# Decay attention with seven quarter products for each pair of query, key and gate tiles, in a two-layer transformer kernel

## The reference, cut to what matters

```python
qkv = silu(hidden_states @ qkv_w.T)            # hidden_states: layernorm(x), K = 512
q, k, v = ...                                  # (b, 32 heads, 1024, 128) each
def step(kv, blk):                             # blocks of the sequence
    scores = einsum('bhnd,bhmd->bhnm', cq, ck) * diag_decay
    intra = einsum('bhnm,bhmd->bhnd', scores, cv)
    inter = einsum('bhnd,bhde->bhne', cq * q_decay, kv)
    kv_next = kv * block_decay + einsum('bhnd,bhne->bhde', ck * k_decay, cv)
    return (kv_next, intra + inter)
xf = attn * rsqrt(mean(attn * attn) + EPS) * norm_w
out = (xf * sigmoid(hidden_states @ gate_w.T)) @ out_w.T      # x = x + out
```

## Time and profile before

| | before |
|---|---|
| median of 3 runs | 3209.59 us (3208.93 to 3212.93) |
| the profiled execution | 3206.87 us, of which 3205.1 us from the first to the last instruction |
| PE busy | 3079.4 us, 96% |
| ACT, DVE, POOL busy | 1341.0, 1272.0, 941.9 us |
| mean granted TensorE clock | 0.981 |
| stage of layer 0 | 0 to 786 us |
| decay attention, batch 0 and 1 | 786 to 1920 us, 1941 to 3076 us |
| routed feed-forward | 3091 to 3205 us |

### The profile page before, as it was taken

The page is one execution under the profiler, slowest core; times in us unless marked ns, Lnnn a source line. Parts: engine busy times, 40 slices in busy tenths (PEclk is TensorE's granted clock), DMA queues, the critical chain, the costliest instruction groups (busy, mean ns, idle before and its releaser), DMA issues. The chain is left out here.

```text
span 3205.1 us, 52455 instructions
## 1 busy us (share of the span) xinstructions
PE 3079.4 (96%) x18776; PEld 2463.2 (77%) x18776; DVE 1272.0 (40%) x2238; ACT 1341.0 (42%) x2342; POOL 941.9 (29%) x747
## 2 busy tenths in 40 slices
PE   7799999889999999999999998999999999999978
PEld 6444444358888888888888887888888888888866
DVE  6677767535222323222222324322222223222268
ACT  5266666644334433333343333333334333333321
POOL 5411111113333332233233323323323332333321
PEclk9699999999999999999999998999999999999989
DMA  4412121010111111111111111111111111111101
GB/s 139 114 26 37 28 38 27 14 37 17 44 48 36 36 36 48 40 36 45 46 36 36 36 36 37 45 44 36 46 46 36 36 36 52 36 39 43 45 20 53
DMA packets 97287, 135.41 MB, mean 42 GB/s; under 512 B 23924, under 2 KB 44148, under 8 KB 97208
## 3 DMA queue, kind: packets, MB, share of 16 engines
q1 hardware_dynamic: 97208, 134.36, 14.7%
HBM read 121.87 MB, written 12.06 MB: 42 GB/s over the span
## 5 line engine op out<-in xcount | busy, mean ns | idle before, releaser
L1624 PE MATMUL bank<-l_xT_hi,l_w_T 128*128 128x512 f32 x3072 | 788.8, 399 | 0.0
L1624 PEld LDWEIGHTS bank<-l_xT_hi,l_w_T 128*128 128x128 f32 x3072 | 556.0, 188 | 104.0
L1554 DVE TENSOR_TENSOR l_sc<-bank,l_mask 128x512 f32<-128x512 f32 x128 | 88.6, 692 | 954.0 <-PE bank L1681 940.9
L1624 PE MATMUL bank<-l_xT_lo,l_w_T 128*128 128x512 f32 x1536 | 412.7, 390 | 0.0
L1425 POOL TENSOR_TENSOR l_w_T<-l_w_raw,l_w_T 128x512 fp32r<-128x512 f32 x192 | 247.9, 1291 | 514.0 <-ACT l_w_T L1468 514.0
L754 ACT ACTIVATE att_exp<-bank 128x512 f32<-128x512 f32 x576 | 322.4, 597 | 175.7 <-PE bank L846 169.1
L791 DVE TENSOR_REDUCE att_max<-bank 128x1 f32<-128x640 f32 (+6 forms) x352 | 346.0, 1026 | 114.2 <-PE bank L831 110.9
L1624 PEld LDWEIGHTS bank<-l_xT_lo,l_w_T 128*128 128x128 f32 x1536 | 288.4, 188 | 63.9
L1624 PE MATMUL bank<-l_o_T,l_y_hi 128*128 128x512 f32 x1024 | 324.1, 393 | 7.3 <-DVE l_y_lo L1527 7.3
L1496 ACT ACTIVATE l_v<-bank 128x256 f32<-128x256 f32 x256 | 98.3, 384 | 489.8 <-PE bank L1624 489.8
L1624 PE MATMUL bank<-l_v_T,l_xT_hi 128*128 128x256 f32 x2048 | 293.8, 284 | 4.4 <-PEq L993 2.7
(11 more groups left out here) (250 smaller groups left out, 4596.0 us busy)
## 6 DMA issues: line engine op xcount, KB each, us to landing
l_w_raw<-in_L_attn_qkv_w SPq DMA_DIRECT2D x198, 256.0 KB, 2.8
l_w_raw<-in_L_attn_gate_w SPq DMA_DIRECT2D x66, 256.0 KB, 2.6
l_o_raw<-in_L_attn_out_w SPq DMA_DIRECT2D x33, 512.0 KB, 3.6
query_parts<-att_exp SPq DMA_DIRECT2D x48, 128.0 KB
att_QT<-query_parts SPq DMA_DIRECT2D x16, 384.0 KB, 5.7
X<-in_L_attn_x SPq DMA_DIRECT2D x4, 1024.0 KB, 10.9
att_QT<-query_parts SPq DMA_DIRECT2D x16, 256.0 KB, 5.7
l_mask<-in_decay SPq DMA_DIRECT2D x32, 128.0 KB, 2.1
```

The source lines that it names most:

```text
L1554: dve.tensor_tensor(sc[:, half(s)].rearrange("p (c n) -> p c n", n=P), ps_a[n % NA][:, :].rearrange("p (c n) -> p c n", n=P), mask[:, h, : ...
L1624: mm = pe.matmul(out, lhs, rhs, start=(n == 0), stop=(n == len(pairs) - 1))
```

## The change

**Products.** A pair of output tiles (queries and keys of one head, "h0" and "h1"; or the gates of both heads, "g") is a matrix of 256 rows by 1024 columns with K = 512. Cut into quarters it took 8 quarter products, 6 matmuls of 128x512 each. Now 7 are taken, after Strassen's scheme in Winograd's form, numbered 1 to 7 in the events ("p", pair, i). The products 2, 4, 5, 3 accumulate in PSUM onto earlier ones. ACT copies product 1 into the tile, and applies silu or sigmoid to 2 from PSUM; DVE reads 7, 6, 4, 5 and 3 from PSUM, adds what lies in the tile already and writes the tile; then ACT applies the function in place, three times for a pair ("made").

**Sums of weights.** For each pair POOL makes four sums of weight quarters, 128x256 each (`sum_quarters`, event "sums"), and then the split has three steps of 512, 256 and 1024 columns ("split", pair, 0 to 2), high part by ACT and low part by POOL. Values and output weights are split as before.

**Sums of rows.** Four combinations of the quarters of `xT` (`xC`, high and low) are made once a batch, by DVE in 14 steps of 128x1024 (`sums_of_rows`), with two helping sums by POOL. `xC` takes the place of `X`. So all rows are stored in DRAM (`X_dram`, 16 DMAs in `project_and_turn`), those of batch 1 are loaded back during the last turn of batch 0, and all again during the last turn of batch 1. The output sum `acc` of batch 0 is stored in DRAM after its turns, and loaded back in the last turn of batch 1 as `acc_back`.

**End.** `add_to_x` of batch 0 moves from the start of batch 1 to its end: ACT scales `acc_back`, POOL adds it to `X` (8 times 128x512), DVE adds batch 1 (8 times) and then counts the statistics of all 16 tiles, where it was 8.

**Banks and order.** Values, products and projections now share 4 banks. The projection is cut into a part "first" (head 0, 3 matmuls for a tile) and a part "project" (head 1, onto the same bank). In `ORDER` the outputs of head 1 now follow each other, and the splits of the next turn stand at other places. Sigmoid functions stand together, so that the function table changes twice a turn and not four times. The `y_hi` and `y_lo` tiles share the places of `kT` and `qT`.

The core of the diff:

```diff
-L1_BANKS = (2, 4, 2)
+L1_BANKS = (4, 4)
+def sum_quarters(nc, pool, w_raw, sums, at, summed, before):
+    a11, a12 = w_raw[:, at, 0:2 * P], w_raw[:, at, 2 * P:4 * P]
+    a21, a22 = w_raw[:, at + 1, 0:2 * P], w_raw[:, at + 1, 2 * P:4 * P]
+    nc.gpsimd.tensor_tensor(sums[:, 0, :], a21, a22, ALU.add).then_inc(summed, 1)
+    nc.gpsimd.tensor_tensor(sums[:, 2, :], a11, a21, ALU.subtract).then_inc(summed, 1)
+    pool.wait_ge(summed, before + 1)
+    nc.gpsimd.tensor_tensor(sums[:, 1, :], sums[:, 0, :], a11, ALU.subtract).then_inc(summed, 1)
+    pool.wait_ge(summed, before + 3)
+    nc.gpsimd.tensor_tensor(sums[:, 3, :], a12, sums[:, 1, :], ALU.subtract).then_inc(summed, 1)
...
+        ORDER = ([("v", t) for t in range(3)] + [("split", "o", 0)] + [("v", t) for t in range(3, 6)]
+                 + [("split", "o", 1), ("sums", "h1"), ("v", 6), ("v", 7)]
+                 + [("p", "h0", 1), ("split", "v", 0), ("p", "h0", 7), ("split", "v", 1), ("p", "h0", 2), ("p", "h0", 6),
+                    ("p", "h0", 4), ("p", "h0", 5), ("made", "h0", 4), ("p", "g", 1), ("turn", 0, 0), ("made", "h0", 5),
+                    ("p", "h0", 3), ("turn", 0, 1), ("made", "h0", 3), ("qd", 0), ("p", "g", 7), ("score", 0, 0),
+                    ("split", "h1", 0), ("p", "g", 2), ("update", 0, 0), ("split", "h1", 1), ("score", 0, 1),
+                    ("p", "g", 6), ("split", "h1", 2), ("p", "g", 4), ("p", "g", 5), ("made", "g", 4), ("update", 0, 1),
+                    ("made", "g", 5), ("p", "g", 3), ("made", "g", 3)]
+                 + [("p", "h1", 1), ("sums", "g"), ("p", "h1", 7), ("out", 0, 0), ("p", "h1", 2), ("high", 0, 0),
+                    ("p", "h1", 6), ("low", 0, 0), ("split", "g", 0), ("p", "h1", 4), ("split", "g", 1), ("p", "h1", 5),
+                    ("made", "h1", 4), ("out", 0, 1), ("made", "h1", 5), ("turn", 1, 0), ("p", "h1", 3), ("high", 0, 1),
+                    ("low", 0, 1), ("made", "h1", 3), ("qd", 1), ("turn", 1, 1), ("split", "g", 2), ("sums", "h0"),
+                    ("score", 1, 0), ("update", 1, 0), ("split", "h0", 0), ("score", 1, 1), ("update", 1, 1),
+                    ("out", 1, 0), ("high", 1, 0), ("low", 1, 0), ("out", 1, 1), ("high", 1, 1), ("split", "h0", 1),
+                    ("split", "h0", 2)]
+                 + [("first", t) for t in range(CH)] + [("low", 1, 1)] + [("project", t) for t in range(CH)]
+                 + [("first", t) for t in range(CH, C)] + [("project", t) for t in range(CH, C)])
+        PAIR_BANKS = {"h0": (0, 1, 2), "g": (3, 0, 2), "h1": (1, 2, 3)}
...
+                        if kind == "high":
+                            n = gated(*event[1:])
+                            pool.wait_ge(sems.sq_ready, HP * H * it + n + 1)
+                            pool.wait_ge(sems.sq_added, CREDIT + HP * H * it + n)
+                            nc.gpsimd.tensor_tensor(sq_sum[:, half(event[2])], sq_sum[:, half(event[2])], sq[:, :],
+                                                    ALU.add).then_inc(sems.sq_added, 1)
...
+                            for n, (w, x, xc, c) in enumerate(terms):
+                                mm = pe.matmul(ps_p[p_bank(event)][:, :],
+                                               w[:, SLOT[pair], LEFT[i], P * c:P * c + P], quarter(i, x, xc, c),
+                                               start=(n == 0 and i in (1, 6, 7)), stop=(n == len(terms) - 1),
+                                               skip_group_check=True)
...
+                if b == BATCH - 1:
+                    pool.wait_ge(sems.rows_in[0], 16)
+                    for t in range(C):
+                        pool.wait_ge(sems.scaled, t + 1)
+                        nc.gpsimd.tensor_tensor(X[:, t, :], X[:, t, :], buf.acc_back[:, t, :], ALU.add
+                                                ).then_inc(sems.whole, 1)
```

More of the change, by code:

```diff
@@ L1238, in linear_attend_semaphores @@
[L1238 to L1266, removed]
@@ new lines @@
+@dataclass
+class DecaySemaphores:
+    w_in: list
+    o_in: object
+    const_in: object
+    p_ready: object
+    p_read: list
+    a_ready: object
+    a_read: list
+    made: object
+    summed: object
+    split_hi: object
+    split_lo: object
+    sp_passed: object
+    qd_ready: object
+    state_ready: object
+    sq_ready: object
+    sq_added: object
+    yhi_ready: object
+    ylo_ready: object
+    cleared: object
+    sum_ready: object
+    rms_step: object
+    root: object
+    added: object
+    counted: object
+    x_out: object
+    x_back: object
+    x_step: object
+    acc_out: object
+    rows_in: list
+    acc_in: object
+    scaled: object
+    whole: object
@@ L1287, in linear_attend @@
         CH = C // H
[L1288 to L1305, removed]
@@ new lines, in linear_attend, with p_bank @@
+        PAIR_BANKS = {"h0": (0, 1, 2), "g": (3, 0, 2), "h1": (1, 2, 3)}
+        IN_P = [e for e in ORDER if e[0] in ("v", "p", "project")]
+        IN_A = [e for e in ORDER if e[0] in ("turn", "score", "update", "out")]
+        MADE = [e for e in ORDER if e[0] == "made"]
+        SUMS = [e for e in ORDER if e[0] == "sums"]
+        SPLITS = [e for e in ORDER if e[0] == "split"]
+        PR, LA = len(IN_P), len(IN_A)
+        assert LA % NA == 0 and len(SPLITS) == TURN_SPLITS
+        def p_bank(event):
+            if event[0] == "p":
+                return PAIR_BANKS[event[1]][{1: 0, 2: 0, 3: 1, 5: 1, 6: 1, 4: 2, 7: 2}[event[2]]]
+            return event[1] % NP_
@@ L1522, in _ @@
+                nc.scalar.activation(rms[:, 1, :], rms[:, 0, :], ACT.Sqrt).then_inc(sems.root, 1)
+                if b == BATCH - 1:
+                    act.wait_ge(sems.acc_in, 16)
+                    for t in range(C):
+                        nc.scalar.mul(buf.acc_back[:, t, :], buf.acc_back[:, t, :], buf.rms[0][:, 2, t:t + 1]
+                                      ).then_inc(sems.scaled, 1)
             @block.vector
             def _(dve):
-                def low_y(it, h, s):
-                    dve.wait_ge(yhi_ready, HP * H * it + gated(h, s) + 1)
-                    dve.wait_ge(y_ready, CREDIT + C * it)
-                    dve.tensor_tensor(y_lo[:, h, half(s)], gT[:, h, half(s)], y_hi[:, h, half(s)],
-                                      ALU.subtract).then_inc(ylo_ready, 1)
```

727 lines of the change are left out of this document (440 added, 287 removed).

## The result

The changed kernel takes 3281.3 us (median of 4 runs, 3278.6 to 3286.5); beside it the kernel before took 3209.3. The ratio is 1.0224 (95% interval 1.0206 to 1.0242): 2.2% slower. I had forecast 3220 us and a range of 3166 to 3250. Of the rivals, the fourth comes nearest: the clock falls behind the new wait in each turn, at 3271.

The account below looks back on a forecast made before the run. PE was taken to bound the kernel, with POOL's queue giving back nearly all the gain: 3206.9 - 7 (turns) + 5 (start) + 13 (end) = 3218 profiled, so a median of 3220.5 us, range 3166 to 3250.

Parts of the forecast that it names:

- rival 4: In each turn the clock falls behind the new 3.3 us wait, costing 1.6 us a turn: 3271 us; chance 0.06.
- PE's own work: In a turn of decay attention, 18 fewer matmuls and 0.4 us less waiting bring PE from 70.8 to 66.3 us.
- The two waits that I had forecast: PE waits in a turn: 0.3 us at ("p", "g", 3) for its bank, 0.7 us at an output for `qd`.
- The chain behind P: At a turn's end POOL's queue delays the fourth square and bank 0: PE waits 3.3 us, turn 70.6 us.
- P: Time at which PE ends the turn's last product, ("p", "h1", 3): 48.7 us from the start of the turn.
- The remaining 24 matmuls: Projection matmuls after the wait for bank 0, at the end of a turn: 5.5 us.
- The start of batch 0: DVE's 14 sums of rows, the first two slowed by POOL, make PE wait 5 us for product 4.
- Between the batches: PE's gap (1920 to 1941) stays and the sums of rows are ready in time: nothing to pay.
- The end: After the turns, DVE and POOL additions alternate for SBUF, then 16 statistics follow: 13 us more.
- `project_and_turn`: Before decay attention, 16 stores and longer splits add 0 to 2 us, taken as 0.
- Rival 1, 2 and 3: A turn of 69.6, 67.1 or 71.7 us through POOL's chain shorter, covered or longer; 3181, 3109, 3256; chances 0.23, 0.08, 0.13.
- Rival 2: The wait for `sq` is covered, so PE bounds the turn at 67.1 us: 3109 us in total; chance 0.08.

Follow-up runs that it names:

- all three edits: Against the changed kernel: POOL's queue reordered, its batch-start work moved to DVE or delayed, its final additions begun after DVE's; 3110.1 us, ratio 0.9696.

## Why the prediction was wrong, step by step

- **PE's own work: right.** I had 66.3 us a turn. In the kernel with all three edits a turn lasts 67.53. The timeline of PE, from two turns:

```profile
945.46 1.64 PE L1865 MATMUL bank<-l_xT,l_w_T 128*128 128x512 f32 x6
947.22 0.52 PE L1895 MATMUL bank<-identity_f,l_kT 128*128 128x128 f32 x3
...
957.15 0.83 PE L1908 MATMUL bank<-l_v,l_kd 128*128 128x128 f32 x6
958.18 1.20 PE L1865 MATMUL bank<-l_xT,l_w_T 128*128 128x512 f32 x4 [0.20 <-DVE l_gT L1760]
...
1854.00 0.83 PE L1908 MATMUL bank<-l_v,l_kd 128*128 128x128 f32 x6
1855.12 0.71 PE L1836 MATMUL bank<-l_sc,l_v 128*128 128x128 f32 x4 [0.29 <-POOL l_qd L1600]
```

By the starts PE is off its pace in three places: 1.76 us for product 3 of h0 in place of 1.47 (0.3, at the second transposes), 1.03 in place of 0.6 at ("p", "g", 3) (0.43), 1.12 in place of 0.59 at `qd` (0.53). Without these 1.26 us it is 66.3. The two waits that I had forecast, 0.3 + 0.7, are 0.43 + 0.53; the one at the transposes I had missed.
- **The chain behind P: right, within 0.7 us at each step.** P at 49.0 us of the turn (forecast 48.7, the missed 0.3), bank 0 free at P + 15.9 (16.4), the wait 2.6 us (3.3), ACT's pause 4.31 (5), released as forecast. POOL's sums take 0.74 (0.75), `y_lo` held up by the lock 1.16 (0.69 alone), `qd` and the split 2.36 each (2.35). In the one turn of the 28 in which the clock holds the changed kernel takes 70.5 us, and with four idle matmuls all 28 do: forecast 70.6. That it comes so near is in part luck, since P came 0.3 us later and the bank 0.5 us sooner behind it.
- **The remaining 24 matmuls: the step that failed.** I put them at 5.5 us, the pace of the full clock, and they take 7.0 (1010.28 to 1017.24). The average turn of batch 0 behind the first is 72.2 us, 1.6 more than the forecast; with batch 1 the turns carry about 45 of the 62 us that the profiled execution lies above 3218; the start of batch 0 carries 6.5, the gap between the batches 5.9, and what comes before the decay attention 4.8. This was rival 4, at the price it had (1.6). My error was its chance: I gave it 0.06 on the strength of one row, 0.73 for the first four matmuls after an idle time of 2.7 us, and read it as a rule for a wait of 3.3. The runs say that it isn't one: after 2.2 us the clock fell in most turns and held in some. Even at the place of that row it isn't one. Behind the same idle time of 2.74 us the values of the first turn took 11.6 us at a granted clock of 1.00 in the kernel before, but 13.0 to 13.1 us in the changed kernel and in all nine experiments (0.59 and 0.56 granted from 791 to 793 and 793 to 795 in the changed one). A single row can't show how often such an event comes. The other row, 0.86 behind the gap, pointed the right way.
- **The start of batch 0: mechanism right, size too small.** Forecast 5 us, measured 11.5 (7.8 of wait, 2.0 of slow clock behind it, 12 matmuls in 4.8 us from 817.90 to 822.69, and 1.4 of slow clock in the values, as said above). DVE's 14 steps took 26.5 us (790.68 to 817.2) for the 21.4 of the forecast, because I let POOL's instructions meet only the first two. POOL's splits and sums of the first turn meet the last eight; each takes 1.6 to 2.3 us there in place of 1.22 (the one CAST 1.75 for 0.69). With POOL kept away there is no such wait.
- **Between the batches: wrong.** I took the gap as unchanged; it grew by 5.9 us. I had looked at what was added behind the gap, not at POOL's instructions in it: the two sums and the memsets are released by the fourth tile of `lo_done`, beside DVE's normalization.
  The Trainium skill, SBUF — State Buffer, section Who interferes with whom, names `tensor_scalar` among the DVE instructions that can take the shared port pair too, in a mode with two ports, and says that the other engine then fully blocks; here the 6.33 us against 0.54 agree with it. That DVE stood through the three memsets queued behind the POOL addition too is what this trace shows. I had used only its sentence on two SBUF inputs, with which the 1.55 us of each addition at the end agree.
- **The end: the mechanism right, the size partly by luck.** 13 forecast, 12.8 measured, with the alternation that the lock makes. But a pair of additions takes 1.55 us and not 1.75, so the eight take 12.4 and not 14; a small DVE step held up by POOL's first addition takes 1.12 us in place of 0.17; and the 14 + 9.7 of the forecast are 23.7, not the 23.2 that I wrote.
- **`project_and_turn`: 0.5 us** more where I took 0 of 0 to 2. It takes 112.0 us in the kernel before, 112.5 to 112.6 in seven of the ten kernels that have the change, and 114.0 in three, this one among them, though its code is the same in all ten. The other 2.8 of the 4.8 us up to there lie in code that wasn't changed; over the ten kernels that code ends between 672.8 and 679.0 us.
- **Rival 1, 2 and 3.** POOL's chain was within 0.5 us of the forecast, neither as short nor as long as the rivals had it. Rival 2's turn of 67.1 us is what the kernel does as soon as the wait for `sq` is covered, in two different ways: 67.5.

## What to carry to other kernels

When a change makes one engine's work shorter, look at each single buffer between it and the others and ask where in the releasing engine's queue the release stands; moving a short release ahead of long work that nobody waits for, or doubling the buffer, was worth 141 us of 3281 here, twice the whole loss. Price a new wait of 2 us or more on PE, in every turn of a loop, with a fall of the clock as a likely case and not as a rare one, and fill it with idle matmuls if it can't be removed. Keep POOL's work away from stretches in which DVE's sums or normalization are what PE waits for, and lay it beside DVE work that it was seen not to slow, such as the statistics here (4.84 us for eight); one input in SBUF alone isn't enough, as the normalization step shows.

## What the runs showed of the hardware that I had not expected

- A wait of PE of 1.7 us never lowered the clock (28 of 28 turns), one of 2.2 us did in 22 of 28 and one of 2.6 us in 27 of 28, for 1.3 to 1.6 us in most (2.8 to 2.9 in three). Seven or eight matmuls then take 0.43 us each instead of 0.23.
- A DVE `TENSOR_SCALAR` with one tile in SBUF stood from 1974.64 to 1980.97, that is until POOL's addition and all three memsets behind it were over, though these began after it. DVE's two-input sums, in contrast, took 1.22 us beside the same memset in the first batch. So the engines meet at SBUF too, and not only at semaphores.
